# ScalarE copies the turned input, and a new frame's turned keys, ahead of the exponentials of a step

## The reference, cut to what matters

```python
for i in range(DEPTH):                       # DEPTH = 6
    x = attn_layer(shift_tokens(x), Wqkv[i], q_scale[i], k_scale[i], Wo[i]) + x
    x = ffn_layer(shift_tokens(x), ln_g[i], ln_b[i], W1[i], b1[i], W2[i], b2[i]) + x

def attn_layer(x, Wqkv, qs, ksc, Wo):
    qkv = x @ Wqkv                            # x: 2048 x 128, Wqkv: 128 x 3072
    q, k, v = jnp.split(qkv, 3, -1)
    q = l2norm(q) * qs
    k = l2norm(k) * ksc
    ...                                       # rotary, scaled by position
    out = local_attention(q, k, v)            # softmax over the own and the previous window
    return out.transpose(0, 2, 1, 3).reshape(b, n, INNER) @ Wo
```

## Time and profile before

| | |
|---|---|
| median of 3 runs | 3019.39 us (3017.44 to 3027.82) |
| the profiled execution's own time | 3019.65 us |
| its span, first to last instruction | 3017.8 us |
| PE busy | 2834.6 us, 94% of the span |
| VectorE, ScalarE, GpSimd busy | 2305.5, 1755.7, 1673.3 us |
| mean granted TensorE clock | 0.986 |

### The profile page before, as it was taken

How to read it: one execution, slowest core, us unless ns; L and a number is a source line. 1 busy time by engine, 2 the same in 40 slices (tenths; PEclk the granted TensorE clock), 3 DMA queues, 4 the chain that set the end, 5 groups by cost and what they waited for, 6 DMA issues and landing times.

```text
span 3017.8 us, 98279 instructions
## 1 busy us (share of the span) xinstructions
PE 2834.6 (94%) x41012; PEld 1861.7 (62%) x41012; DVE 2305.5 (76%) x3660; ACT 1755.7 (58%) x2615; POOL 1673.3 (55%) x1459
## 2 busy tenths in 40 slices
PE   6999999999999999889999999999999999999996
PEld 6555556555666665556656666666666666666664
DVE  2777765585577776988867888788888888788883
ACT  1555555555666665555566666566666666666653
POOL 0000001100366665666667888778887888788872
PEclk7999999999999999999999999999999999999998
DMA  2000000000011211243233434333433343333332
GB/s 93 1 1 1 1 1 1 3 1 10 11 47 45 46 46 29 78 125 80 67 105 98 97 80 110 80 92 91 117 91 83 86 110 88 90 91 84 83 76 55
DMA packets 181657, 188.21 MB, mean 62 GB/s; under 512 B 77598, under 2 KB 128548, under 8 KB 179684
## 3 DMA queue, kind: packets, MB, share of 16 engines
q1 hardware_dynamic: 181220, 181.94, 24.0%
HBM read 60.99 MB, written 6.03 MB: 22 GB/s over the span
## 4 chain that ended last, share of the span: by engine, by line
PE 75%; DVE 10%; issue 6%; POOL 3%; SPq 3%; ACT 3%; DMA 1%; DVEq 0%; ACTq 0%; POOLq 0%
PE ps L1359 15%; PE ps L594 12%; PE ps L1367 5%; PE ps L1410 5%; PE ps L1452 5%; PE ps L1374 4%; PE ps L629 4%; PE ps L607 4%; PE ps L1473 2%; PE ps L1419 2%; PE ps L541 2%; PE ps L1466 2%; PE ps L1400 2%; PE ps L612 2%; DVE nmx L701 2%
## 5 line engine op out<-in xcount | busy, mean ns | idle before, releaser
L1359 PE MATMUL ps<-wqkv,xcT 128*128 128x512 f32 x1152 | 558.0, 607 | 52.5 <-issue 33.9
L594 PE MATMUL ps<-xnT,qp 128*128 128x512 f32 (+3 forms) x1280 | 528.4, 544 | 16.3 <-ACT prob L819 15.5
L1980 POOL TENSOR_TENSOR ra<-ra,rb 128x1024 f32<-128x1024 f32 x191 | 450.8, 2366 | 121.9 <-DVE rb L1842 121.1
L819 ACT ACTIVATE prob<-ps,ebias,shift 128x1024 f32<-128x1024 f32 (+7 forms) x384 | 360.7, 955 | 144.0 <-DVE ebias L710 75.7
L827 ACT ACTIVATE probT<-ps 128x512 f32<-128x512 f32 (+3 forms) x384 | 207.9, 541 | 352.1 <-PE ps L607 351.9
L594 PEld LDWEIGHTS ps<-xnT,qp 128*128 128x128 f32 x1280 | 232.6, 191 | 274.3 <-issue 226.9
L1999 POOL TENSOR_TENSOR ra<-ra,rn 128x1024 f32<-128x1024 f32 x192 | 362.3, 1908 | 8.9 <-DVE ra L1907 1.2
L1359 PEld LDWEIGHTS ps<-wqkv,xcT 128*128 128x128 f32 x1152 | 196.0, 190 | 220.2 <-issue 208.7
L701 DVE TENSOR_REDUCE nmx<-ps 128x1 f32<-128x1024 f32 (+7 forms) x256 | 245.9, 987 | 111.2 <-PE ps L594 96.2
L1621 ACT ACTIVATE sq<-ps 128x1024 f32<-128x1024 f32 x192 | 195.5, 1018 | 90.7 <-PE ps L1359 90.6
L1840 DVE TENSOR_TENSOR ra<-ps,tab 128x1024 f32<-128x1024 f32 x192 | 233.5, 1216 | 3.9 <-issue 3.5
(11 more groups left out here) (279 smaller groups left out, 5673.4 us busy)
## 6 DMA issues: line engine op xcount, KB each, us to landing
vw<-vs SPq DMA_DIRECT2D x576, 130.0 KB
vw<-vs SPq DMA_DIRECT2D x384, 65.0 KB
bc<-bc_scratch SPq DMA_DIRECT2D x128, 128.0 KB, 3.1
area<-bc_scratch SPq DMA_DIRECT2D x128, 128.0 KB, 4.4
wqkv<-lwqkv_dram SPq DMA_DIRECT2D x6, 1536.0 KB, 8.8
xc<-xs SPq DMA_DIRECT2D x96, 32.0 KB
wo<-lwo_dram SPq DMA_DIRECT2D x6, 512.0 KB, 9.5
area<-ys SPq DMA_DIRECT2D x24, 128.0 KB
```

What stands on the lines that cost most here:

```text
L594: mm = E.matmul(ps[:, 2 * r + o // 512, 0:w], k.qp[:, group % 2, g % NTH * P:(g % NTH + 1) * P], k.xnT[:, k0 + o:k0 + o + w], start=True, ...
L819: A.activation(k.prob[:, r, 0:nk], ps[:, 2 * r:2 * r + 2, :].rearrange("p a b -> p (a b)")[:, 0:nk], ACT.Exp, bias=k.ebias[:, row % 2:row ...
L1359: mm = E.matmul(to[:, c, :], k.xcT[:, n % 4, :], k.wqkv[l % 2][:, at + 512 * c:at + 512 * (c + 1)], start=True, stop=True)
L1980: G.tensor_tensor(k.ra[:, n % 2, w, :], k.ra[:, n % 2, w, :], k.rb[:, w, :], ALU.add).then_inc(s("added_" + what), 1)
```

## The change

In each step of ScalarE's loop the copy of the turned input (`turned_input(n + 3)`) and, in frame steps, the copy of the turned keys (`halo_turned(n + 1)`) stand ahead of the two exponentials (`probs(n)`) and the keys' squares (`square("k", n + 2)`). Before, they stood behind both. Nothing else is changed: no instruction is added or taken away, and PE's, VectorE's, GpSimd's and SyncE's streams are the same.

```diff
@@ -1752,14 +1752,14 @@
         for u in units(n + 1):
             A.wait_ge(s("chunk"), 32 * (u // NS - NCH // 2 + 1))
             unit_decay(k, u)
+        if n + 3 < NTILE:
+            turned_input(n + 3)
+        if new_frame(n + 1) and n + 1 < NTILE:
+            halo_turned(n + 1)
         if n < NTILE:
             probs(n)
         if n + 2 < NTILE:
             square("k", n + 2)
-        if n + 3 < NTILE:
-            turned_input(n + 3)
-        if new_frame(n + 1) and n + 1 < NTILE:
-            halo_turned(n + 1)
         if n == 0:
             norm_squared()
         if n + 1 < NTILE:
```

## The result

The changed kernel takes 2989.18 us (median of 4 runs, 2986.91 to 2990.64) against 3020.42 us for the kernel before (4 runs): a ratio of 0.9888, with a 95% interval of 0.9873 to 0.9904. The profiled execution took 2990.14 us, 29.5 less than that of the kernel before. The forecast was 2972: the sign and the place are right, and the gain is some two thirds of the 47.8 us that the sum gave.

What follows compares the result with a forecast made beforehand. PE, busy 94% of the span, was taken to set the pace. Step gains of 52.7 us, less 4.4 for late DMAs and 0.5 for the copy, gave 47.8 us off 3019.65 us: 2972 us, range 2960 to 2995.

Steps and rivals of the forecast that it cites:

- the sum: Whole kernel: step gains of 52.7 us, less 4.4 and 0.5, give 47.8 us.
- What "issue" ahead of L1359 was: PE's unnamed idle time ahead of the values' projection is a wait for ScalarE's late copies, 49.8 of 52.5 us.
- The constant 0.10 us: In plain steps the values' projection begins 0.10 us behind the end of copy L1629, so that copy releases it.
- The rival that "issue" is PE's own time: At L1359 only the 19 named waits go: gain 18.4 us, 3001 us; chance 0.05.
- The copy's cost ahead of the exponentials: On ScalarE: nothing where it idles, 0.8 us of cover beyond; 0.5 us in all, in steps 17 and 18.
- The next limit: At L1410, VectorE's copy L1860 has 0.68 us of cover in step 42, so 0.58 of 0.62 us can be had.
- the 4.4 and 0.5 for transfers and late exponentials: Deductions: 4.4 us for SyncE's late DMAs of the values, 0.5 us for the copy in steps 17 and 18.
- The 64 other plain steps give 0.58 each: 37.1 us: Plain steps not set by VectorE's chain, apart from 17 and 18, each gain 0.58 us, 37.1 us together.
- The frame steps, 13.0 + 1.9 us: Thirteen frame steps with room give 1.0 us each, 13.0 us; five bound by L1860 give 1.9 us.
- Nine plain steps give nothing: Steps where VectorE's chain through the exponentials sets PE's pace and L1860 already ends 0.10 us ahead of L1410: no gain.
- if PE comes 0.6 us earlier, a wait is left and VectorE moves along: VectorE's wait for L1410 ahead of its normalisations, 1.6 us a step, lets a step's gain reach the end.
- VectorE and GpSimd meet more often: Rival at VectorE's scans: 24 more blocked scans of 0.96 us cost 23 us, 2995 us; chance 0.06.

Runs made afterwards that it cites:

- the two one-input profiles: VectorE's 128 scans replaced by one-input reductions, recurrence left out: on the kernel before 3023.97 us, on the changed kernel 2975.84 us.
- the first relief: VectorE's scans replaced by reductions over one SBUF input; ratio 0.9997 on the kernel before, 0.9834 on the changed kernel.
- the second: Copy L1860 of the turned probabilities moved from VectorE to ScalarE: on the kernel before 3017.67 us, on the changed kernel 2961.32 us.
- the reduction: The kernel before with VectorE's scans replaced by a reduction over a doubled view of one SBUF operand: 3023.97 us.

## Why the prediction was right, and where its size was off

**What "issue" ahead of L1359 was: right.** The constant 0.10 us read as a release was one. L1359's idle time fell from 52.5 to 6.0 us, and the gap in step 42 shrank by the 0.62 us that was worked out. The rival that "issue" is PE's own time fails for L1359; the breaks within L1374 and L1410 are no wait for another engine. What the prediction got wrong here are the other releases of the pair. It looked at `ys` alone and took "0.32 us in step 57" for an exception; in 57 the projection begins 0.21 us behind the end of VectorE's L1873 in both kernels, and in 39 and 75 the same L1873 ended 0.17 us ahead of the frame's copy, which hid it.

**The copy's cost ahead of the exponentials: right** as far as the time can tell. Between the exponentials and the squares it gives the same time. L1400's waits for the exponentials did grow, from 9.2 to 12.9 us, but with the copies behind the exponentials they are 13.1 us, so the copies are not what makes them.

**The next limit: right in its place.** In 79 of the steps 0 to 93 L1410 now starts 0.10 us behind L1860, in 9 before. With this copy moved, the change's worth is 56.4 us. The sum without this limit would have been 64.7, less the 4.4 and 0.5 for transfers and late exponentials: 59.8.

**The sum: wrong by 18 us,** 47.8 against the 29.5 of the profiled pair. Of the 18, 2.2 lie ahead of the first values of step 0 and 2.6 behind step 94. What lies ahead can't be put down to the change: the changed kernel reaches its first L1410 2.2 us later than the kernel before, but the two one-input profiles reach it 3.7 and 4.7 us earlier than kernels that have the same code there, so two profiles differ by that much. The rest, 13.5, is in steps 1 to 94. Step by step, three terms are 18 us too high (less the 4.9 us taken off for transfers and late exponentials, and with 0.3 us lost in steps 93 and 94, that is the 13.5):
- "The 64 other plain steps give 0.58 each: 37.1 us". They gave 27.1. Four of them make 7.0 of the missing 10: steps 38, 41, 57 and 72 became 4.7 us longer instead of 2.3 shorter. PE's new idle times in them are breaks within groups in 38 (0.45 and 0.82 us) and 57 (0.84), the 1.19 us wait for `vw` and a break (0.46) in 41, and 1.23 us of "issue" ahead of L1359 in 72. The last stands at one of the stream's places too, and PE goes on 1.5 us behind the end of its instruction packet, so it looks like one more of the breaks. Step 57 also keeps its gap of 0.67 us, the wait for L1873.
- The frame steps, 13.0 + 1.9 us. They gave 11.2. Eleven of the 13 with room gave 11.1 us, as foretold; the other two, 39 and 75, gave 0.2 instead of 2.0, since L1873 holds the projection there. The five bound by L1860 gave -0.1 instead of 1.9, and in four of them the scans are long.
- "Nine plain steps give nothing". They gave -4.4: steps 31, 47 and 63 -0.5 to -0.6 each, all three with long scans, with waits of L1400 for the exponentials that rose from 0.2 or 0.3 us to 0.8, and with a new 0.66 us ahead of L1410; step 6 -1.6, where L1400 waits 2.59 us, 2.19 before; steps 2 and 12 -0.7 and -0.5.

**The step of the argument that failed** is "if PE comes 0.6 us earlier, a wait is left and VectorE moves along". VectorE does, until it meets GpSimd. In the steps with long scans these end no earlier against GpSimd's L497 and L499, as step 47 shows, and its chain (scans, maximum, subtraction, exponentials, L1400, L1860) then sets the step. The old order hid this: there the wait for `xcT` takes over as soon as the scans are short, as step 47 shows with one-input scans. Three pairs of kernels bear it out. The change is worth 31.2 us with the kernel's own scans and copies, 48.1 with scans that GpSimd can't hold, and 56.4 with a VectorE that has 1.2 us a step less to do; and the first relief is worth nothing in the old order, the second 8.3. The prediction had this as a rival, "VectorE and GpSimd meet more often", 2995 us, at 0.06, and priced it as 24 more blocked scans of 0.96 us, 23 us. The scans did become 16.1 us longer in sum, and relieving them returned 13.3 us. That is more than these steps lost against the forecast: the five frame steps, 31, 47 and 63 fell short by 3.7 us, with 27 and 79 by 5.3. With short scans they gain beyond the forecast, which had taken their late VectorE as given. So the 13.3 us are a limit on the change's worth, and not a share of the missing 18. As a second outcome beside the main one it should have had much more than 0.06, and been a term of the sum: "as many may be freed" was a guess, and the rows of step 43 in the kernel before (its scans are long there too) would have shown that the scans' end hangs on L497 and L499.

**Transfers: too high.** 4.4 us were taken off. The new profile has one wait for `vw`, 1.2 us in step 41, and none in step 73, where 0.93 stood; there the last of the ten transfers is issued 15.75 us behind the start of the values' projection of step 72, 17.12 before. The break of 1.23 us had made PE late against SyncE's queue just ahead of that projection, so the wait was spared by luck.

**What stays open.** The breaks within groups add up to 8.7 us more in the changed kernel (26.2 against 17.5), which is part of the plain steps' shortfall in this pair of profiles. But the "issue" of L1374, most of it, is 12.8 us in the kernel before, 14.4 with only L1860's copy moved, 18.1 with the reduction and 20.2 with only the frame's copy moved, all with L1359 still waiting, against 14.5 to 19.3 in kernels without that wait. So one profile each cannot tell how much of it the change brought, and the breaks are an untested rival for a part of the shortfall; that the two reliefs of VectorE return 17 and 25 us of the change's worth is from medians of several runs, and stands without it. Nor was it tried to put GpSimd's L497 elsewhere, which would test the hold on the scans from its other side, nor was L1873 moved ahead in VectorE's order.

## What to carry to other kernels

A wait that an in-order engine causes hides the waits behind it: price the next limit in the steps where another engine's chain is nearly as long, not only in the typical step. Where that chain holds an instruction that a third engine can block, see what its end hangs on (here each scan's end, 0.55 us behind that of a GpSimd instruction), since such an end doesn't move when the engine comes earlier. Where a wait covers several releases, list all of them and look at the steps that have the rare ones: one left out here cost 2.4 us in three steps. And once a change has moved the limit, try again what was worth nothing before: the same move of one copy gained 8 us ahead of the change and 28 behind it.

## What was not expected of the hardware

PE breaks off within groups of small matmuls that wait for nothing, for 0.1 to 2.8 us, at places 125.33 matmuls apart in its stream; not at each of them, and the length of a break varies. Adding 60 instructions leaves the places where they were. At each of these breaks PE goes on 1.2 to 1.6 us behind the end of an instruction packet of 16384 bytes, one for each place. These breaks take 17 to 26 us in each of the kernels here.

Two scans of VectorE that take 1.38 us when undisturbed took up to 3.3 beside GpSimd. The first ended 0.55 us behind GpSimd's L497 and the second 0.55 us behind L499, so the pair ended 2.16 to 2.18 us behind L497, however early it had begun: so it is in the 12 of 64 pairs of the kernel before that took over 2.6 us, and in the 14 of the changed kernel. Of these pairs 1 took over 3.2 us before, and 11 after the change.
